# Two cross-attention and feed-forward layers on one core: context and value weight loaded ahead of X, two more value projections as plain float32 products, one warming product, and new order tables

## The reference

```
x += attn0(LN(x), ctx)   # q = LN(x) Wq, k,v = ctx [Wk|Wv]: 32 query heads of 16, 8 key/value heads; softmax over keys; then Wo
x += ffn0(LN(x))         # LN(x) W^T + bias + a low-rank adapter picked by batch
x += attn1(LN(x), ctx)   # 16 heads of 32, biases; its softmax runs over batch*head (axis 0), not over keys
x += ffn1(LN(x))         # LN(x) (W_base + a low-rank term through an inverse real FFT)^T + bias
```

## Time and profile before

| | |
|---|---|
| median of 3 runs | 298.01 us (297.05 to 298.06) |
| the profiled execution, its own time | 297.65 us |
| its span in the trace | 295.9 us |
| PE busy in the span | 290.2 us (98%), 2192 products |
| DVE, ACT, POOL busy | 232.1, 162.2, 146.9 us |
| DMA | 33.10 MB, 112 GB/s on average |

### The profile page before, as it was taken

How to read it: one execution, slowest core, us unless ns; L and a number is a source line. 1 busy time by engine, 2 the same in 40 slices (tenths; PEclk the granted TensorE clock), 3 DMA queues, 4 the chain that set the end, 5 groups by cost and what they waited for, 6 DMA issues and landing times.

```text
span 295.9 us, 6338 instructions
## 1 busy us (share of the span) xinstructions
PE 290.2 (98%) x2192; PEld 229.8 (78%) x2192; DVE 232.1 (78%) x374; ACT 162.2 (55%) x276; POOL 146.9 (50%) x193
## 2 busy tenths in 40 slices
PE   6999999999999999999999999999999999999996
PEld 2788776856875675688998998898996778888885
DVE  5689787798968975366594966889978799989772
ACT  5957767873388257744437256463745367443220
POOL 6784304270338031225130285386388849998451
PEclk9999999999999999999999999999999999999999
DMA  7956376318034421001433142441444612000112
GB/s 252 351 155 232 112 231 221 107 40 311 31 126 145 142 73 41 0 2 31 139 106 95 52 141 52 125 116 45 128 150 111 210 42 69 2 3 35 73 71 106
DMA packets 32137, 33.10 MB, mean 112 GB/s; under 512 B 3609, under 2 KB 21273, under 8 KB 32107
## 3 DMA queue, kind: packets, MB, share of 16 engines
q1 hardware_dynamic: 32106, 32.70, 35.4%
HBM read 18.39 MB, written 2.10 MB: 69 GB/s over the span
## 4 chain that ended last, share of the span: by engine, by line
PE 91%; POOL 4%; DVE 1%; issue 1%; ACT 1%; POOLq 0%; ACTq 0%; DVEq 0%
PE ps L490 18%; PE ps L492 17%; PE ps L491 17%; PE ps L755 5%; PE ps L665 5%; PE ps L835 4%; PE ps L722 3%; PE ps L744 3%; PE ps L763 3%; PE ps L874 3%; PE ps L847 2%; PE ps L772 1%; PE ps L885 1%; PE ps L919 1%; PE ps L678 1%
## 5 line engine op out<-in xcount | busy, mean ns | idle before, releaser
L1225 DVE TENSOR_REDUCE mx<-ps 128x8 f32<-128x1024 f32 x32 | 37.9, 1218 | 4.2 <-PE ps L722 4.0
L1438 POOL TENSOR_SCALAR var_eps<-moments 128x1 f32<-128x1 f32 x32 | 7.1, 222 | 67.9 <-DVE moments L1187 67.0
L1426 POOL TENSOR_TENSOR slot_l<-stg,slot_h 128x512 fp32r<-128x512 f32 x19 | 26.1, 1386 | 21.9 <-ACT slot_h L943 21.9
L490 PE MATMUL ps<-xT_h,slot_h 128*128 128x256 f32 x128 | 36.9, 289 | 0.0
L1022 ACT ACTIVATE PT<-ps 128x1024 f32<-128x1024 f32 x32 | 31.7, 1023 | 8.8 <-PE ps L744 8.7
L492 PE MATMUL ps<-xT_h,slot_l 128*128 128x256 f32 x128 | 36.0, 281 | 0.0
L491 PE MATMUL ps<-xT_l,slot_h 128*128 128x256 f32 x128 | 36.0, 281 | 0.0
L490 PEld LDWEIGHTS ps<-xT_h,slot_h 128*128 128x128 f32 x128 | 24.2, 189 | 2.0 <-issue 0.6
L1468 POOL TENSOR_TENSOR zpart<-P 128x512 f32<-128x512 f32 x16 | 21.3, 1330 | 7.2 <-ACT P L1089 6.3
L491 PEld LDWEIGHTS ps<-xT_l,slot_h 128*128 128x128 f32 x128 | 24.2, 189 | 0.3
L492 PEld LDWEIGHTS ps<-xT_h,slot_l 128*128 128x128 f32 x128 | 24.2, 189 | 0.0
(11 more groups left out here) (173 smaller groups left out, 851.9 us busy)
## 6 DMA issues: line engine op xcount, KB each, us to landing
ctx_in<-in_ctx SPq DMA_DIRECT2D x20, 256.0 KB, 3.4
QS<-Q_h SPq DMA_DIRECT2D x16, 256.0 KB, 2.9
Q<-Q1d SPq DMA_DIRECT2D x64, 64.0 KB, 2.0
X<-in_x SPq DMA_DIRECT2D x8, 256.0 KB, 4.3
stg<-in_wq SPq DMA_DIRECT2D x8, 256.0 KB, 4.1
QS<-Q_l SPq DMA_DIRECT2D x8, 256.0 KB, 3.0
out<-XB SPq DMA_DIRECT2D x7, 256.0 KB, 2.0
KS<-K_h SPq DMA_DIRECT2D x8, 128.0 KB, 2.4
```

What stands on the lines that cost most here:

```text
L490: eng.matmul(dst, left[0], right[0], start=start, stop=False)
L1225: dve.tensor_reduce(mx[:, b % 2, :].rearrange("p (x r) -> p r x", r=REP)[:, r, :], wide(step).rearrange("p k (g t) -> p (k g) t", g=4), AX ...
L1426: pool.tensor_tensor(lo, src, hi.bitcast(F32), ALU.subtract).then_inc(w_lo_pool, 1)
```

## The change

Apart from the tables, three things change: `WARM` goes from 3 to 1, `PLAIN` from two batches to four (so `CT.0.2`, `CT.0.3`, `CL.0.2` and `CL.0.3` are gone from the tables), and the first `ST` steps on ACT wait for the readers of PT as these now are. All five tables are laid out anew from the first step to the last, with the same steps but for those four. A line or two of each table stands in the diff, the rest is left out:

```
-WARM = 3
+WARM = 1
...
 SP_TEXT = """
-LX.0 LX.1 LC.0.0 LW.wkv.0 LI LW.wkv.1 LC.0.1 LW.wq0.0 LW.wq0.1 LW.wq0.2 LX.2 LW.wq0.3 LC.0.2 LX.3 LX.5 LC.0.3 LX.4
+LC.0.0 LW.wkv.0 LW.wkv.1 LC.0.1 LX.0 LI LX.1 LC.0.2 LC.0.3 LW.wq0.0 LX.2 LW.wq0.1 LW.wq0.2 LW.wq0.3 LX.3 LX.7 LX.4
...
 PE_TEXT = """
-XT.0.1:4 XT.0.0:7 V0.0:0 V0.1:1 Q0.0.0:5 K0.0:0 Q0.0.1:6 MX.0.1:4 MX.0.0:0 V0.2:3 MX.0.3:6 MX.0.2:4 XT.0.3:2 V0.3:3
+V0.1:3 V0.0:1 XT.0.0:2 XT.0.1:7 V0.3:4 K0.0:2 Q0.0.0:3 Q0.0.1:1 MX.0.1:2 MX.0.0:4 V0.2:7 MX.0.3:1 MX.0.2:4 XT.0.3:6
...
 ACT_TEXT = """
-SET.8 W.wkv.0 LNn.0.0 W.wkv.1 XT.0.1 XT.0.0 W.wq0.0 W.wq0.1 W.wq0.2 V0.0 W.wq0.3 V0.1 CT.0.2 K0.0 Q0.0.0 CT.0.3
+W.wkv.0 SET.8 V0.1 LNn.0.0 V0.0 W.wq0.0 XT.0.0 XT.0.1 W.wq0.1 W.wq0.2 V0.3 W.wq0.3 K0.0 Q0.0.0 Q0.0.1 LNn.0.3
...
 DVE_TEXT = """
-SET.6 LNs.0.0 LNs.0.1 LNn.0.1 L.wkv.0 XT.0.1 XT.0.0 C0 L.wq0.1 LNs.0.2 LNs.0.3 K0.0 CL.0.2 Q0.0.0 LNs.0.4 MX.0.1
+SET.6 LNs.0.0 C0 LNs.0.1 LNn.0.1 LNs.0.2 XT.0.0 XT.0.1 L.wq0.1 LNs.0.3 K0.0 Q0.0.0 L.wkv.0 LNs.0.4 LNs.0.5 MX.0.1
...
 POOL_TEXT = """
-SET.1 SET.2 SET.0 LNs.0.0 LNs.0.1 L.wkv.1 L.wq0.0 L.wq0.2 L.wq0.3 KM.0 LNs.0.2 LNs.0.3 CL.0.3 KM.1 LNs.0.4 L.wo.2
+SET.2 SET.1 SET.0 LNs.0.0 LNs.0.1 L.wq0.0 L.wq0.2 L.wq0.3 KM.0 LNs.0.3 KM.1 LNs.0.2 LNs.0.5 LNs.0.4 L.wkv.1 LNs.0.7
...
-PLAIN = (("V0", 0), ("V0", 1))
+PLAIN = tuple(("V0", b) for b in range(4))
...
                     elif g2 == 0:
-                        all_filled(act, PLAIN)
+                        all_filled(act, PLAIN[:2])
                         for c in range(2):
                             chunk_split(act, ("wkv", c))
                     elif g2 == 1:
-                        for early_b in AHEAD:
-                            ctx_split(act, 0, early_b)
+                        all_filled(act, PLAIN[2:])
```

More of the change, by code:

```diff
@@ new lines @@
+LW.lb.0 LC.0.6 LC.0.7 LS QL.3 LW.w0.1 DM.3 LW.w0.0 LC.1.0 LW.la.0 KL.2 QL.4 LW.wk1.0 QL.5 DM.4 LC.1.1 DM.5 LW.wk1.2
+LC.1.3 KL.3 LW.wk1.3 QL.6 LW.wk1.1 QL.7 DM.6 LW.wq1.0 DM.7 LW.wq1.3 LW.wq1.1 LC.1.2 LW.wq1.2 QX.1 QX.0 QX.3 QX.2
+LC.1.4 QX.5 LC.1.5 QX.4 LW.wv1.2 QX.6 LE QX.7 LC.1.7 LL LW.wv1.0 LC.1.6 LW.wv1.3 LW.wv1.1 QX.8 QX.9 QX.10 LW.dft.3
+QX.11 LW.dft.2 QX.13 QX.12 LW.dft.1 LW.dft.0 QX.14 QX.15 LC.2.4 LW.wbase.2 LB LW.wbase.3 LW.wbase.1 LC.2.5 LC.2.2
+LW.wbase.0 LC.2.3 LC.2.0 LC.2.1 OUT.6 OUT.7 OUT.4 OUT.5 OUT.2 OUT.3 OUT.0 OH.1.1 OH.1.0
@@ L89 @@
-W.wbase.1 V1.4 V1.3 V1.2 PV1.6 CT.2.1 PV1.7 PV1.4 V1.0 FP.0 PV1.5 LNn.3.6 V1.1 XT.3.6 LNn.3.7 PV1.2 PV1.3 LNn.3.4
-XT.3.7 PV1.1 XT.3.4 PV1.0 LNn.3.3 XT.3.5 XT.3.2 XT.3.3 XT.3.0 XT.3.1
+W.wkv.0 SET.8 V0.1 LNn.0.0 V0.0 W.wq0.0 XT.0.0 XT.0.1 W.wq0.1 W.wq0.2 V0.3 W.wq0.3 K0.0 Q0.0.0 Q0.0.1 LNn.0.3
+LNn.0.2 XT.0.3 V0.2 XT.0.2 MT.0 LNn.0.4 K0.1 W.wo.0 W.wkv.1 Q0.1.0 ST.0.1 ST.0.0 ST.0.3 W.w0.2 ST.0.2 XT.0.5 XT.0.4
+C0 Q0.1.1 MT.1 W.wo.2 CT.0.4 CT.0.5 PV.0.0 Q0.2.0 ST.1.0 PV.0.1 ST.1.3 ST.1.2 MT.2 ST.1.1 Q0.2.1 PV.1.1 PV.1.0
@@ L121 @@
+LNs.1.7 LNs.2.3 LNs.2.2 LNs.1.6 ZP.0 ZP.1 LNs.2.4 LNs.2.5 CL.1.4 ZP.2 ZP.3 LNs.2.6 LNs.2.7 ZP.4 ZP.5 L.wv1.2 ZP.6
+ZP.7 ZP.8 ZP.9 ZP.10 ZP.11 ZP.12 ZP.13 CL.2.4 ZP.14 ZP.15 CL.2.2 CL.2.3 NM.13 CL.2.0 L.wbase.1 L.wbase.3 CL.2.1
+L.wbase.0 L.wbase.2 NM.4 LNs.3.6 LNs.3.7 NM.3 XB.6 LNs.3.4 NM.1 XB.7 LNs.3.5 LNs.3.2 XB.4 LNs.3.3 XB.5 LNs.3.0 XB.2
+LNs.3.1 XB.3 XB.0 XB.1
 """
```

111 lines of the change are left out of this document (51 added, 60 removed).

## The result

The changed kernel takes 301.6 us (median of 4 runs, 300.59 to 303.24), the kernel before 298.03 (4 runs, 297.05 to 298.19): a ratio of 1.0132 with a 95% interval of 1.008 to 1.0184. It is slower by 3.6 us, and lies above the predicted range of 297.0 to 301.0. The profiled execution took 301.22 us with a span of 299.4, against 297.65 and 295.9 before.

What follows compares the result with a forecast made beforehand. PE's products were taken to bound the kernel from 12.01 us on, with 0.64 us idle in all. Costs of 0.55 + 0.45 + 0.35 = 1.35 us on 297.65 gave 299.0 us, range 297.0 to 301.0.

Steps and rivals of the forecast that it cites:

- Before, at equal content ... PE would be there at 13.65: First query product: before's 12.01 plus K0.0 (0.15) and split V0.3 (1.48) is 13.65; against 14.2, cost +0.55 us.
- The forecast's own sign of an error: PE's later stretch differing by more than 1 us from before, less what moved ahead of it, would show the forecast wrong.
- PE's 0.64 us of idle time: From 12.01 us on PE idles 0.64 us in all, so relief of ACT, DVE or POOL gives at most some 0.6.
- The clock, and V0.1: Start: full rate from 7.8 us, 4.1 after the first product; V0.1 runs from 6.4 to 8.9 us.
- The chain of the start: Loads, V0.1, V0.0, X's transposes, V0.3, K0.0 and the query weight: first query product at 14.2 us.
- the clock starts to count at V0.1 only: Rival: clock up at 10.5 us, first query product at 15.55, kernel 300.35 us; chance 0.3.
- "wq0" second piece, +0.45: First query step: the query weight's second piece is ready at 16.1 us, wanted at 15.65, cost +0.45 us.
- V0.2 plain, +0.35: V0.2 as a plain step takes 1.83 instead of 1.48 us of PE where PE has no gap: +0.35 us.
- The rest of the tables. I take 0: Remaining steps in new order: may win back up to 0.64 us or open like waits; taken as 0, 1 us either side.

Runs made afterwards that it cites:

- fourteenth kernel: The fifth kernel (before, four plain value steps) with V0.3 moved forward alone, behind K0.0 and ahead of Q0.0.1: 299.79 us, ratio 1.0078.
- experiment 15: The changed kernel with V cleared first, three warming products, and DVE's L.wkv.0 moved from ahead of the first maxima to behind XT.0.2: 300.38 us, ratio 1.0082.
- experiment 16: The kernel of experiment 15 with V0.3 back at its old place behind XT.0.3 on PE (bank 3) and K0.0 in bank 4: 303.73 us, ratio 1.0154.
- kernels 6: The changed kernel, still with one warming product, with V0.3 moved back behind V0.2 on PE and ACT: 303.36 us, ratio 1.0197.
- kernel 7: The changed kernel with three warming products, V0.3 behind V0.2, and ACT's W.wq0.0 ahead of V0.0: 302.41 us, ratio 1.0138.
- kernel 13: The changed kernel with three warming products, V0.3 behind V0.2, K0.0 in bank 4, W.wq0.0 ahead of V0.0, L.wkv.0 behind XT.0.2: 302.33 us, ratio 1.0155.
- third kernel: The changed kernel with V cleared ahead of KS and three warming products: 300.08 us, ratio 1.0062.
- fifth kernel: The kernel before with four plain value steps in their old places and the four context splits taken out: 298.09 us, ratio 1.0000.
- Experiments 1 and 2: First: head of before up to XT.0.2, changed tables behind, 298.17 us. Second: head of the changed kernel, tables of before behind XT.0.2, 303.02 us.
- 9: The third kernel with two DVE steps moved later, L.wkv.0 behind XT.0.2 and LNs.0.5 behind MX.1.0: 306.3 us, ratio 1.0268.

## Why the prediction was wrong

The sum was +1.35 us over the comparison at 13.65 us; the last product of the changed kernel comes 3.54 us later than before. By its own steps:

**"Before, at equal content ... PE would be there at 13.65": this step failed, and is the largest error, 1.48 us.** It credits the changed kernel with V0.3, as if each product that is done early shortened what comes later. It does not: "to MT" is 6.01 in the fourteenth kernel and 6.05 in the fifteenth without V0.3, and 6.02 in the kernel before with it. DVE's maxima set that stretch, and V0.3 had run in their shadow. The forecast's own sign of an error says the same: PE's stretch from the first query product to its last product's end takes 281.25 us, against 281.17 before less the 1.63 us moved ahead, 1.7 us more where it allowed 1. I had argued from PE's 0.64 us of idle time that relief of DVE gives nothing, which is right, and had let it stand for the reverse too. PE without a gap does not mean that PE sets the pace; DVE without a gap from 18.60 to 23.82 us stood in the same trace, unread. This shadow belongs to the order of before: in the changed order V0.3 at its old place costs 1.43 us more (7.48 for 6.05, experiment 16), and in kernels 6, 7, 13 and 16 PE waits at the place that it left, 1.3 to 1.8 us, for DVE's work on the transposed X. What was moved ahead is a filling of a longer start (whether the loads moved back make it longer, no run shows alone): 14.28 us to the first query product with a good clock, for 12.01 before.

**The clock, and V0.1: a term mis-sized.** The chain of the start is right in kind and order, and 1.27 us too short (15.47 for 14.2). Context block 1 was 0.5 us later than its place in the queue had said. Then the clock: I took 7.8 us, 4.1 us after the first product, and it rose near 9.6; V0.1 took 3.06 us for 1.83 at the full rate and lost 1.23 us where I had 0.7, which makes another 0.54. The last 0.2 us lie behind V0.0, 3.67 us to the first query product for 3.45 in the forecast. The third kernel gives 1.2 us of span and 1.5 us of time back by the clock alone. The rival "the clock starts to count at V0.1 only" named the right place and almost the right time for the first query product, 15.55, though by a clock at 10.5; that agreement is in part luck.

**"wq0" second piece, +0.45: not seen.** The first query product came late enough, and DVE's rest of that piece took 1.11 us and not 1.48 (15.44 to 16.55), ahead of the 16.9 us at which it was wanted.

**V0.2 plain, +0.35: hidden.** The duration is as forecast (1.87 us to the next step that is ready), but the fifteenth kernel with V0.2 plain reaches MT.0 in 6.05 us and the kernel before with the split one in 6.02. PE waited for DVE behind it in the changed kernel anyway. The fifth kernel's time agrees, though by its interval alone 0.35 us could not be excluded.

**"The rest of the tables. I take 0": half right.** Experiments 1 and 2 show that the order behind XT.0.2 is neutral to a few tenths of a us. The order of DVE within the first 30 us is not: `wkv_l` ahead of the first maxima costs 0.84 us in its stretch (experiment 15). How much of it is in the kernel's time stays open, as removing it moved the loss elsewhere. Behind Q0.1.0 the changed kernel is 0.54 us shorter than before, inside my allowance of 1 us; which wait gave that was not traced.

Put together from 1.35, as bookkeeping of two profiled executions and not as a separate measurement of each term: +1.48, +1.27, +0.84, less 0.80 for the two terms that did not appear, less 0.54 later, makes 3.6, against the 3.57 us between the two profiled executions.

## What to carry to other kernels

An engine that shows no gap is not by that the one that sets the pace: before crediting work that is moved out of a stretch, see whether another engine is gapless in the same stretch, because then the work may have been done under the other's cover, and moving it may be worth nothing. Such a cover holds for one order of the steps: here it was there before, and not in the changed order. Moving one input forward in a queue moves others back, and if what the next stage waits for comes no sooner (here the transposed X and the query weight), early work only fills the wait. In this kernel three warming products up to the first real work were worth 1.5 us (300.08 for 301.6) over one with a gap behind it.

## What was not expected of the hardware

The granted clock in the windows reads 1.00 before the first recorded change, while the loads of equal products stand at twice their later spacing (0.43 us for four up to 9.47 in the changed kernel). At the start only the spacing tells.

With three warming products the full rate came anywhere from 4.9 to 7.8 us, with one from 9.6 to 11.3. It differs between kernels whose warming products stand the same, so that the start of any one profiled execution is uncertain by about a microsecond.

Short waits were followed by a fall to 1.2 GHz: in kernel 7 behind 1.3 us of waiting (1.2 GHz from 14.58 to 17.99 us), in 16 behind 1.8 (15.21 to 18.62), in 9 with waits of 1.0 and 2.2 (34.05 to 40.88), and in 14 behind waits of 1.5 and 0.6 (9.90 to 13.32). In the profiled execution of kernel 13 a wait of 1.5 us was not followed by one, though another of its four, 303.62 us at a mean granted clock of 0.994, seems to have had one. Nor is it the same in each execution of the other kernels: going by the mean clock (0.994 or less) it came in 2 of 4 of kernel 7, 3 of 4 of 9, 2 of 10 of 14 and 3 of 4 of 16. What a wait costs here can be more than its length, and these runs don't tell in advance when.
